# Keeping the hi and lo turned rows of all sixteen token tiles in memory from the first shared pass, and loading them back for the six shared jobs behind it

## The reference, cut to what matters

```python
h = _layernorm(x) * (1 + cb) + sb
scores = softmax(h @ gate_weight.T);  topk_w, topk_idx = top_k(scores, 2)     # 8 experts
y  = sum over the 2 chosen experts e of w_e * (silu(h @ w_gate[e].T) * (h @ w_up[e].T)) @ w_down[e].T
y += (silu(h @ sw_gate.T) * (h @ sw_up.T)) @ sw_down.T      # shared, 704 wide = 2 x 352
x  = x + gb * y
```

## Time and profile before

| What | Value |
| --- | --- |
| Median of three runs | 1524.89 us |
| The profiled execution's own time | 1526.7 us |
| Its span, first to last instruction | 1524.5 us |
| PE matmul busy | 1502.2 us, 99% of the span |
| DVE, ACT, POOL busy | 64%, 48%, 47% |
| Granted TensorE clock, mean | 0.998 of full speed |
| Mean DMA rate | 205 GB/s |
| Chain that ended last | PE 85%, DMA 4%, POOL 4%, DVE 3%, issue 2%, ACT 1%, SP's sequencer 1% |

### The profile page before, as it was taken

How to read it: one execution, slowest core, us unless ns; L and a number is a source line. 1 busy time by engine, 2 the same in 40 slices (tenths; PEclk the granted TensorE clock), 3 DMA queues, 4 the chain that set the end, 5 groups by cost and what they waited for, 6 DMA issues and landing times.

```text
span 1524.5 us, 29262 instructions
## 1 busy us (share of the span) xinstructions
PE 1502.2 (99%) x8812; PEld 1340.2 (88%) x8812; DVE 983.0 (64%) x2213; ACT 729.5 (48%) x1733; POOL 713.5 (47%) x767
## 2 busy tenths in 40 slices
PE   8999999999999999999999999999999999999997
PEld 4788888887999999999999999988999899999986
DVE  5977666677777777777777777785458322222258
ACT  4532222346666666666666666663332233333323
POOL 1113333446766665666565665769822211111054
PEclk9999999999999999999999999999999999999999
DMA  9336555577858486666757485746543555765576
GB/s 321 125 139 228 193 194 193 210 265 239 252 171 247 141 255 184 202 182 208 216 164 231 145 244 165 234 161 225 196 163 140 199 201 190 282 233 194 195 230 226
DMA packets 205600, 311.92 MB, mean 205 GB/s; under 512 B 80641, under 2 KB 142465, under 8 KB 198609
## 3 DMA queue, kind: packets, MB, share of 16 engines
q1 hardware_dynamic: 198400, 287.04, 56.6%
q0 software_dynamic: 5680, 18.62, 4.1%
q10 hardware_dynamic: 1440, 5.24, 0.9%
HBM read 189.97 MB, written 120.88 MB: 204 GB/s over the span
## 4 chain that ended last, share of the span: by engine, by line
PE 85%; DMA 4%; POOL 4%; DVE 3%; issue 2%; ACT 1%; SPq 1%; POOLq 0%; another core or an unknown queue 0%; ACTq 0%; DVEq 0%
PE bank L1624 45%; PE bank L1738 17%; PE bank L1853 7%; PE bank L1805 7%; PE bank L1836 4%; PE bank L1907 2%; PE bank L1941 1%; DMA h<-slot_results,pos_i 1%; DMA mod_early<-wmod 1%; POOL acc L1071 1%; POOL acc L1069 1%; DMA keys<-k_ring 1%; DMA ffn_rows<-h 1%; DMA w<-experts_lo 0%; DMA xr<-x 0%
## 5 line engine op out<-in xcount | busy, mean ns | idle before, releaser
L1624 PE MATMUL bank<-w,xt 128*128 (+2 forms) x1608 | 287.5, 327 | 0.3 <-ACT gate_s L1552 0.2
L1624 PEld LDWEIGHTS bank<-w,xt 128*128 128x128 f32 x1608 | 261.9, 188 | 6.6 <-DVE xt L2271 0.6
L1448 ACT ACTIVATE prob<-prob,row_inv 128x128 f32<-128x128 f32 (+3 forms) x256 | 137.3, 560 | 78.5 <-DVE row_inv L2308 78.3
L2427 DVE TENSOR_TENSOR ht_lo<-bank,ht_hi 128x128 fp32r<-128x128 f32 (+1 forms) x213 | 48.4, 282 | 181.0 <-ACT ht_hi L1567 176.4
L1436 ACT ACTIVATE prob<-bank,neg_max 128x128 f32<-128x128 f32 (+3 forms) x256 | 133.8, 526 | 42.3 <-DVE neg_max L2300 42.1
L1624 PE MATMUL bank<-wv_hi,h_hi 128*128 128x256 f32 x512 | 147.1, 287 | 0.0
L1624 PE MATMUL bank<-w,ht_hi 128*128 (+3 forms) x426 | 138.7, 406 | 6.8 <-DVE ht_lo L2427 5.9
L1624 PE MATMUL bank<-wv_hi,h_lo 128*128 128x256 f32 x512 | 144.7, 283 | 0.0
L1624 PE MATMUL bank<-wv_lo,h_hi 128*128 128x256 f32 x512 | 144.7, 283 | 0.0
L1248 POOL DMA_INDIRECT xin<-ffn_rows,slot_tokens x39 | 39.8, 1019 | 185.1 <-PE bank L1907 181.4
L2295 DVE TENSOR_REDUCE row_max<-bank 128x1 f32<-128x128 f32 (+3 forms) x256 | 119.7, 488 | 6.6
(11 more groups left out here) (252 smaller groups left out, 3882.7 us busy)
## 6 DMA issues: line engine op xcount, KB each, us to landing
keys<-k_ring SPq DMA_DIRECT2D x64, 512.0 KB, 3.2
ch_raw<-wexp SPq DMA_DIRECT2D x128, 170.0 KB, 3.2
experts_hi<-ch_hi SPq DMA_DIRECT2D x128, 170.0 KB, 2.6
experts_lo<-ch_lo SPq DMA_DIRECT2D x128, 170.0 KB, 2.8
w<-experts_hi SPq DMA_DIRECT2D x9, 2176.0 KB, 7.8
w<-experts_lo SPq DMA_DIRECT2D x9, 2176.0 KB, 14.5
q_transposed<-q_out SPq DMA_DIRECT2D x64, 256.0 KB, 2.1
k_even<-keys SPq DMA_DIRECT2D x16, 1024.0 KB, 5.7
```

Source lines behind the costliest of these rows:

```text
L1448: ins = act.activation(part, part, ACT.Copy, scale=row_inv[:, h, r:r + 1])
L1624: ins = pe.matmul(dst, a, m, start=(k == 0), stop=(k == last))
```

## The change

All sixteen tiles' turned rows are stored in jobs 0 to 15 instead of the last ten. Jobs 16 to 21 load them, in the slots 2, 0, 1, 2, 0, 1, instead of loading plain rows and turning them. So six `turn_rows` (16 to 21) leave PE, six `xt_part` leave ACT and DVE, six `load_xin` of 256 KB leave SP; six stores of 512 KB on ACT's queue and six loads of 512 KB on SP's queue are added. ACT's wait for the store of tile n - 2 now begins at tile 2. The load for job 61 moves from ahead of the routed slots to behind slot 37. Counters that skip the six tiles step by seven at tile 22. PE's loop over jobs 4 to 15 ends at 13; jobs 14 and 15 are written out.

The pieces below are, in order: the slots; SP's list (two pieces); ACT's `xt_part` and its store; PE's `half` and its calls of `job`.

```diff
+            if isinstance(n, int) and NT <= n < R0:
+                return (2, 0, 1)[(n - NT) % 3]
             return 2 - (n - Z0) % 3 if isinstance(n, int) and n >= Z0 else s
...
+            def load_xt(m):
+                sp.wait_ge(up_full, m - 2)
+                if m == NT:
+                    sp.wait_ge(xt_hi_ok, 4)
+                elif m == NT + 1:
+                    sp.wait_ge(xt_st, 16 * NT)
+                sem_, _ = loaded_xt(m)
+                sp.dma_start(xt_of(m, 0).bitcast(F32).rearrange("p w c n -> p (w c n)"),
+                             xt_d[m - NT if m < R0 else NB1 + m - Z0]).then_inc(sem_, 16)
...
-            for m in range(14, NT + 4):
-                load_xin(m)
+            load_xin(14)
+            load_xin(15)
+            load_xt(NT)
+            load_xt(NT + 1)
+            load_xt(NT + 2)
             sp.wait_ge(y_full, NT)
             load_w(0, 0)
-            for m in range(NT + 4, R0):
-                load_xin(m)
+            for m in range(NT + 3, R0):
+                load_xt(m)
...
-            sp.wait_ge(xt_st, 16 * NB2)
-            sp.dma_start(xt_of(Z0, 0).bitcast(F32).rearrange("p w c n -> p (w c n)"), xt_d[0]).then_inc(loaded_xt(Z0)[0], 16)
...
+            load_xt(Z0)
             load_xt(Z0 + 1)
             routed(NSLOT - 1, 0)
...
             def xt_part(n, s):
                 act.wait_ge(xt_full, n + 1)
-                if isinstance(n, int) and NB1 + 2 <= n < NT + 2:
-                    act.wait_ge(xt_st, 16 * (n - 1 - NB1))
+                if isinstance(n, int) and 2 <= n < NT:
+                    act.wait_ge(xt_st, 16 * (n - 1))
...
-                if isinstance(n, int) and NB1 <= n < NT:
+                if isinstance(n, int) and n < NT:
                     store_xt(n, s)
...
                 if which == 0:
-                    pe.wait_ge(*(loaded_xt(n) if isinstance(n, int) and n >= Z0 else (xt_ok, n + 1)))
+                    kept = isinstance(n, int) and (NT <= n < R0 or n >= Z0)
+                    pe.wait_ge(*(loaded_xt(n) if kept else (xt_ok, n + 1)))
...
-            job(NT, 0, W1, 0, free=(y_gb, NT - 2), prev_at=WDA)
+            job(NT, 0, W1, 0, nxt=False, free=(y_gb, NT - 2), prev_at=WDA)
...
-                job(n, n % 2, W1, W1, free=(y_gb, n - 2),
+                job(n, n % 2, W1, W1, nxt=n + 1 == R0, gathered=n + 1 == R0, free=(y_gb, n - 2),
```

More of the change, by code:

```diff
@@ L236, in adaln_layer @@
         y_d = dram("slot_results", (NSLOT * P, D))
-        xt_d = dram("turned_rows", (NB2, P, 2 * D))
+        xt_d = dram("turned_rows", (NT, P, 2 * D))
         bank = [ctx.enter_context(nc.psum_tensor(f"bank{i}", [P, T], F32)) for i in range(8)]
@@ L627, in loaded_xt @@
         def loaded_xt(m):
-            k = xt_slot(m, 0)
-            return (xin_ld + xt_ld)[k], (0 if k == 2 else R0 * 8) + (m - Z0) // 3 * 16 + 16
+            k, rows = xt_slot(m, 0), 16 * (NT // 2)
+            use = (m - NT) // 3 if m < R0 else NB1 // 3 + (m - Z0) // 3
+            return (xin_ld + xt_ld)[k], (0 if k == 2 else rows) + use * 16 + 16
         def finished(i):
@@ L954, in store_y @@
                 sp.dma_start(y_t[:, bass.ds(r, 1), :], y_sb[:, s, :].unsqueeze(1)).then_inc(y_st[s], 16)
[L956 to L961, removed]
             def store_out(i):
@@ L1246, in gather_x @@
                 n = r + R0
-                pool.wait_ge(xt_full, n - 1)
+                pool.wait_ge(xt_full, NT + 1 - R0 + n - 2 if isinstance(n, int) and n < R0 + 2 else n - 1)
                 pool.indirect_dma_start(
@@ L1524, in store_xt @@
             def store_xt(n, s):
-                act.dma_start(xt_d[n - NB1], xt[:, s].bitcast(F32).rearrange("p w c n -> p (w c n)")).then_inc(xt_st, 16)
+                act.dma_start(xt_d[n], xt[:, s].bitcast(F32).rearrange("p w c n -> p (w c n)")).then_inc(xt_st, 16)
             def c_rows(b, t):
@@ L1537, in xt_part @@
                 act.wait_ge(xt_full, n + 1)
-                if isinstance(n, int) and NB1 + 2 <= n < NT + 2:
-                    act.wait_ge(xt_st, 16 * (n - 1 - NB1))
+                if isinstance(n, int) and 2 <= n < NT:
+                    act.wait_ge(xt_st, 16 * (n - 1))
                 act.activation(xt_hi[:, s], bank[2][:, :].rearrange("p (c n) -> p c n", c=DC), ACT.Copy)\
-                   .then_inc(xt_hi_ok, 1)
+                   .then_inc(xt_hi_ok, R0 + 1 - NT if isinstance(n, int) and n == R0 else 1)
             walk_steps(act, step)
@@ L1591, in _ @@
             for n in range(NT):
-                job(n, n % 2, "shared" if n else None, n > 0, route=True)
+                job(n, n % 2, "shared" if n else None, 0 < n < NT - 1, route=True)
                 if n in ROWS_AT:
@@ L1600, in _ @@
             for n in range(NT, R0):
-                job(n, n % 2, "shared", True)
+                job(n, n % 2, "shared", n + 1 == R0)
             job(R0, 0, "shared", True)
@@ L1904, in turn_rows @@
                 if not (isinstance(n, int) and n == 0):
-                    pe.wait_ge(xt_ok, n)
+                    pe.wait_ge(xt_ok, NT if isinstance(n, int) and n == R0 else n)
                 for c in range(DC):
                     ins = pe.transpose(bank[2][:, c * P:(c + 1) * P], xin[:, s, c * P:(c + 1) * P], ident[:, :])
-                ins.then_inc(xt_full, 1)
+                ins.then_inc(xt_full, R0 + 1 - NT if isinstance(n, int) and n == R0 else 1)
             def loaded(m, s, gathered):
@@ L1994, in _ @@
             job(3, 1, 0, 0, route=True, free=(y_gb, 1), prev_at=WDA)
-            with pe.Fori(2, NT // 2) as j:
+            with pe.Fori(2, NT // 2 - 1) as j:
                 for k in range(2):
                     job(j * 2 + k, k, 0, 0, route=True, free=(y_gb, j * 2 + (k - 2)), prev_at=WDA)
+            for n in range(NT - 2, NT):
+                job(n, n % 2, 0, 0, route=True, nxt=n + 1 < NT, free=(y_gb, n - 2), prev_at=WDA)
             for k in range(3):
@@ L2419, in xt_part @@
                 dve.wait_ge(xt_hi_ok, n + 1)
-                low(xt_lo[:, s], bank[2][:, :].rearrange("p (c n) -> p c n", c=DC), xt_hi[:, s], None, xt_ok)
+                dve.tensor_tensor(xt_lo[:, s], bank[2][:, :].rearrange("p (c n) -> p c n", c=DC),
+                                  xt_hi[:, s].bitcast(F32), ALU.subtract)\
+                    .then_inc(xt_ok, R0 + 1 - NT if isinstance(n, int) and n == R0 else 1)
             walk_steps(dve, step)
@@ L2474, in shared_job @@
             def shared_job(n, after_xt=None, after_mid=None, after_ht=None):
-                job(n, n % 2, "shared" if n else None, n > 0, b_prev=(n - 1) % NT // TT, after_xt=after_xt,
+                turned = 0 < n < NT - 1 or n + 1 == R0
+                job(n, n % 2, "shared" if n else None, turned, b_prev=(n - 1) % NT // TT, after_xt=after_xt,
                     after_mid=after_mid, after_ht=after_ht)
```

## The result

The changed kernel takes 1528.57 us (median of 20 runs, 1525.94 to 1534.1); the kernel before took 1525.85 us beside it (20 runs, 1522.97 to 1527.18). The ratio is 1.0021 [1.0014, 1.0027]: slower, since the whole interval lies above 1, though its low end is under the 0.2% that a run can tell from no change. The prediction had 1.6 us less; measured are 2.7 us more, outside its range (1521.4 to 1526.3, likeliest 1523.3).

A forecast was written before the change was run, and what follows sets the result against it. PE, busy 99% of the span, was taken to bound the kernel. Gather -1.9, stores +0.15 and job 61 +0.1 summed to -1.6 us; against the median 1524.89 that gave 1523.3 us, range 1521.4 to 1526.3.

The forecast's parts named there:

- The wait at job 19: Job 19's gate waits 1.5 us (ends 0 and 2.7) for turned rows loaded behind 4352 KB of weights.
- the 0.44 of job 15: In job 15 the split is done before the up matmuls end, so PE gains 0.44 us from the removed transposes.
- The stores: ACT's added stores of tiles 0 to 5, tile 0's issued after the gate's activation at 1034.62: net cost 0.15 us.
- the rule of turns: ACT's tile 0 store shares engines with SP's transfers, landing near 1040.5; down weights move from 1040.9 to about 1042.2.
- a line in order of issue: ACT's tile 0 store queues behind SP's low down weights and 256 KB of rows, landing at 1042.8.
- job 2's gate: Job 2's gate, behind the store of tile 0, starts at 1044.2 against 1043.21: 1.0 us late.
- What job 7 gives back: At job 7 PE has 0.68 us of idle plus 0.17 of pipeline gap to absorb the early delay.
- Job 16: In job 16 PE, 0.44 us early, waits from 1144.40 to about 1144.85 for the low split: transposes become a wait.
- The gather: In job 21 gathered rows land at 1182.4 instead of 1184.27; turning tile 22 moves to about 1182.45, gaining 1.9 us.
- Job 61: Its load, issued at 1444.20, 4.3 us before its gate, costs 0.1 us (ends 0 and 1.9); no PE wait.
- The slower rival: `mods` goes ahead of tile 0's store, job 2's gate starts 3.4 us late: +0.7, 1525.6 us; chance 0.18.
- The first rival: Job 19's load does not stall PE, or by under 0.3 us: gain 3.3 - 0.25, 1521.8 us; chance 0.17.

The follow-up runs named there:

- the last pair: Kernel before with six added stores at new places, 1525.66 us, beside changed kernel with job 19's load ahead, tile 0 stored in job 1, tile 2 in job 3, 1523.42 us.
- the stores alone: Kernel before with only the six stores of tiles 0 to 5 and their wait added, nothing loaded from them: 1527.12 us, ratio 1.0011.
- rows ahead: Changed kernel with job 19's load of turned rows issued ahead of the first expert's weights: 1525.0 us, ratio 0.9998.
- the stores moved: On the changed kernel with job 19's load ahead: tile 0 stored in job 1, tile 2 in the third slot and stored in job 3; 0.9984 in both runs.
- the extra matmuls: Changed kernel with ten matmuls, results unused, added on PE ahead of job 19's gate: 1527.43 us (1.0005), again 1526.1 us (1.0004).
- group 3: Runs on one chip beside the kernel before, including the changed kernel, 1529.76 us (1.0029), and it with ten matmuls added ahead of job 19's gate, 1526.1 us (1.0004).

## Why the prediction was wrong, by its steps

The sum by the runs: -2.2 (transposes and gather, the last pair) + 1.8 (early stores, the stores alone) + 2.9 (the load for job 19, rows ahead or not) = +2.5 us, against +2.7 measured between the medians. Each term is uncertain by more than 1 us; that the sum comes out this near is in part luck. The prediction had 3.3 of gain, 1.4 of it lost again to job 19, 0.15 to the stores and 0.1 to job 61. So the gain was somewhat less than forecast, and two costs were far too small.

- **The wait at job 19: right in place and cause, too small by its second half.** PE was as early as forecast: in the kernel with rows ahead the gate starts 12.86 us after SP's issue of the low weights of the first expert (1149.70 to 1162.56), against 13.61 before (1148.09 to 1161.70), which with the 0.44 of job 15 makes 1.2, forecast 1.1. The wait was 2.21 instead of 1.5, because the low weights ahead took 14.0 us and not 13.2; the 1.2 us of the rows behind them were as forecast (1.25). The larger miss is what followed: 1.68 us lost to the lower clock, in all four profiles with the wait, which the prediction did not have at all. Beside its 1.4 us of lost gain stand 2.85 us measured. This is the first step that failed.
- **The stores: wrong.** The prediction placed the issue of the store of tile 0 behind the gate's activation, 1034.62, because it stands there in ACT's program. It was issued at 1032.94, ahead of the low down weights, and these took 1.8 us longer. The profile before could have warned: there a store is issued at 1075.71, 0.02 us after the start of the activation ahead of it, which ran for 0.60 us. The prediction weighed the rule of turns between rings (the Trainium skill, "DMA: Bandwidth & Descriptors", section "Queues, rings and completion order") by which each DMA engine takes turns between the rings that have work, and set it aside for a line in order of issue. By the rule of turns it had the store land near 1040.5 and the low weights at about 1042.2; they landed at 1041.2 and 1042.16. The trace agrees better with that rule, for the high weights, issued ahead of the store, were slowed as well (5.6 us, before 4.4). Cost 1.8 us between medians instead of 0.15. This is the second step that failed. That job 2's gate was late by 1.4 us, near the forecast 1.0, is luck: ACT waited for the store as forecast, but PE was held by the weights.
- **What job 7 gives back.** Counted from the start of job 0's gate, tile 8 was turned after 52.39 us (1030.68 to 1083.07), before after 51.73: about 0.7 of the 1.4 stayed. The wait of job 7 went, as forecast, but it had only that to give.
- **Job 16, right:** the transposes turned into a wait of 0.36 us on the low split (forecast about 0.45). No transposes ran between 1132.10 and the turning of tile 22.
- **The gather, right in kind:** its wait fell from 1.32 to 0.3 us. But tile 22 was turned 154.90 us after the start of job 0's gate (1030.68 to 1185.58), before 153.44, where the prediction had 151.57 (1182.45 - 1030.88). Of the miss of 3.3 us the steps above make 2.9: 0.5 of the stores, 0.7 of the longer wait, and 1.68 of the clock. Without these costs the gain was near the forecast or a little below it: with the rows ahead and the stores moved, tile 22 came after 150.26 and 151.05 us in two profiles, 3.2 and 2.4 us earlier than before (forecast 3.3).
- **Job 61, right:** SP issued its load at 1446.19 and its gate began at 1450.47 with no wait.
- **The slower rival** had the right queue and the wrong neighbour: it let `mods` go ahead of the store, and PE's job 2 wait for the store. In the trace the store went ahead, and PE waited for weights.
- **The first rival** (no stall at job 19, gain about 3.05) did not occur. Moving the load made its condition true, but the stores' cost then still stood: 0.9998. With the stores moved as well the gain was 2.5 to 2.7 us.

Open: the extra matmuls brought 3.66 us side by side, where the account above gives 1.4 (1.68 of the clock, less the 0.24 by which 2.45 us of work exceed 2.21 of waiting). Up to the turning of tile 22 the two profiles of that group differ by 1.2 us (154.62 and 153.39 us from the start of job 0's gate), as the account has it; the rest lies behind it, where both kernels do the same. There, from the turning of tile 22 to job 61's gate, the fourteen profiles took 264.2 to 266.1 us without order by kernel. Part of the 3.66 is therefore likely scatter: over all groups the changed kernel averages a ratio of 1.0022 and the one with extra matmuls 1.0005, 2.6 us. But in the mean of the runs of group 3 the clock does differ by as much as the time (0.9952 and 0.9975, 0.0023 x 1526 = 3.5 us). What was lost besides the 1.7 us at job 19, in job 1 or at the start, is not known.

## What to carry to other kernels

A new wait of PE can cost more than its length: price behind it a stretch at the lower clock (here 1.7 us behind each wait of about 2 us at job 19, and behind three of seven in job 1), and either issue the load ahead of the large transfers or give PE something to do. A DMA on ACT's queue can be issued ahead of the activation before it in the program (here by 1.48 us), so look in the trace where such stores really go out, and ask not what it costs its engine but which transfers it delays. And before giving up a change that removes work, look for the one or two issues that ate the gain: here three moved issues turned 1.0021 into 0.9984.

## What was not expected of the hardware

- Behind a wait of 1.9 to 2.2 us at job 19 the granted clock fell to 1.2 GHz in four of four profiles, and it was low when PE was already at work again (gate 3.28 us instead of 2.07). But behind a wait of similar length in job 1 it fell in three of seven: 1.00 in the stretch from 1040 to 1050 behind 2.33 us in one profile of the changed kernel, 0.83 behind 2.36 in another.
- ACT's queue issued a store 1.48 us before the activation ahead of it in the program ran (1032.94 and 1034.42), with the loading of a table, 1.28 us, between them.
- 512 KB issued on ACT's queue between two transfers of 768 KB on SP's queue made both slower: the one issued 0.23 us before it by 1.2 us, the one issued 0.25 us behind it by 1.8 us. The 512 KB took 8.2 us themselves. The other two profiles of the changed kernel are alike (5.4 us where it was 4.4 before, 8.9 and 9.1 where it was 7.1, and 8.5 and 8.6 for the store).
